# Cross-attention and quantised FFN on one core: another order of the front, and unread transposes of the identity on TensorE

## What is computed

```
x = x + Wo @ attention(q = Wq @ layernorm(x) + bq, k = Wk @ ctx + bk, v = Wv @ ctx + bv) + bo
        # scores over D x D for each head, scaled by 1/8, softmax over the last axis
x = x + (silu(h @ gate) * (h @ up)) @ down,    h = layernorm(x)
        # gate, up: 512 x 1792, down: 1792 x 512, each (int - zero) * scale by groups of 128 rows
```

## Time and profile before

| | us |
|---|---|
| median of 3 runs | 454.9 (454.37 to 455.94) |
| the profiled execution | 455.48 |
| its span in the trace | 453.7 |
| first `gate_up` starts at | 55.88 of the span |
| PE / DVE / ACT / POOL busy | 408.0 / 326.9 / 332.7 / 269.4 |

### The profile page before, as it was taken

One profiled execution on the slowest core, in us unless ns is written; L12 is line 12 of the kernel. 1 busy time (PEld: TensorE's weight loads), 2 busy tenths in 40 slices (PEclk: granted clock), 3 DMA queues, 4 the chain that ended last, 5 costly groups with the idle time before them and its releaser, 6 DMA issues.

```text
span 453.7 us, 10637 instructions
## 1 busy us (share of the span) xinstructions
PE 408.0 (90%) x4178; PEld 318.2 (70%) x4178; DVE 326.9 (72%) x581; ACT 332.7 (73%) x538; POOL 269.4 (59%) x264
## 2 busy tenths in 40 slices
PE   3566598899798799999999989999999999999994
PEld 2544365677575577777787777877778888888873
DVE  2857623899687776878887756877877666666676
ACT  2135579788687678877867958877878999888970
POOL 3263387779859665666555655656556555555561
PEclk9998579999999999999999989999999999999998
DMA  5985243768374100000201000000000000000003
GB/s 176 360 297 174 93 125 102 255 206 259 128 232 140 62 2 9 17 25 2 73 25 48 0 1 25 2 25 1 25 26 24 0 1 1 23 25 23 24 1 92
DMA packets 27139, 35.50 MB, mean 78 GB/s; under 512 B 2218, under 2 KB 18770, under 8 KB 27090
## 3 DMA queue, kind: packets, MB, share of 16 engines
q1 hardware_dynamic: 26642, 34.76, 23.2%
q10 hardware_dynamic: 320, 0.07, 0.1%
q0 software_dynamic: 128, 0.00, 0.0%
HBM read 30.63 MB, written 4.19 MB: 77 GB/s over the span
## 4 chain that ended last, share of the span: by engine, by line
PE 66%; POOL 11%; issue 9%; DVE 7%; ACT 4%; DMA 2%; SPq 0%; POOLq 0%; DVEq 0%; ACTq 0%
PE banks L708 19%; PE banks L710 17%; PE banks L721 9%; PE banks L722 9%; PE banks L612 3%; POOL t_sb L406 3%; POOL hr L419 2%; PE banks L630 2%; DVE yT L933 2%; PE banks L622 2%; DMA x_sb<-in_x 2%; POOL hr L415 1%; PE banks L641 1%; PE banks L652 1%; ACT banks L529 1%
## 5 line engine op out<-in xcount | busy, mean ns | idle before, releaser
L529 ACT ACTIVATE banks<-banks,ratio 128x512 f32<-128x512 f32 x336 | 208.5, 665 | 37.6 <-PE banks L710 26.8
L708 PE MATMUL banks<-xT,wgu 128*128 128x512 f32 x448 | 184.0, 411 | 5.1 <-DVE t_sb L918 2.7
L933 DVE SCALAR_TENSOR_TENSOR yT<-banks,sd,yT 128x512 f32<-128x512 f32 x208 | 154.5, 747 | 45.7 <-PE banks L722 45.4
L710 PE MATMUL banks<-xT,wgu 128*128 128x512 f32 x448 | 176.6, 394 | 0.0
L406 POOL TENSOR_TENSOR t_sb<-t_sb,u_sb 128x512 f32<-128x512 f32 x56 | 72.9, 1302 | 94.4 <-DVE t_sb L918 94.2
L708 PEld LDWEIGHTS banks<-xT,wgu 128*128 128x128 f32 x448 | 85.2, 190 | 27.5 <-issue 2.9
L721 PE MATMUL banks<-hr,wd 128*128 128x512 f32 x224 | 90.0, 402 | 9.0 <-DVE yT L933 5.6
L710 PEld LDWEIGHTS banks<-xT,wgu 128*128 128x128 f32 x448 | 85.3, 190 | 15.5
L722 PE MATMUL banks<-hr,wd 128*128 128x512 f32 x224 | 87.9, 393 | 0.0
L419 POOL TENSOR_TENSOR hr<-t_sb,hr 128x512 fp32r<-128x512 f32 x56 | 72.1, 1288 | 5.1 <-ACT hr L551 0.7
L721 PEld LDWEIGHTS banks<-hr,wd 128*128 128x128 f32 x224 | 42.2, 188 | 25.2 <-DVE yT L933 13.3
(11 more groups left out here) (80 smaller groups left out, 376.9 us busy)
## 6 DMA issues: line engine op xcount, KB each, us to landing
x_sb<-in_x SPq DMA_DIRECT2D x16, 256.0 KB, 5.4
out<-x_sb SPq DMA_DIRECT2D x16, 256.0 KB, 2.3
wgu_in<-in_L_ffn_gate_w SPq DMA_DIRECT2D x7, 512.0 KB, 6.7
z_in<-in_L_ffn_gate_z SPq DMA_DIRECT2D x7, 512.0 KB, 4.7
wgu_in<-in_L_ffn_up_w SPq DMA_DIRECT2D x7, 512.0 KB, 6.4
z_in<-in_L_ffn_up_z SPq DMA_DIRECT2D x7, 512.0 KB, 4.6
wd_in<-in_L_ffn_down_w SPq DMA_DIRECT2D x7, 512.0 KB, 5.5
z_in<-in_L_ffn_down_z SPq DMA_DIRECT2D x7, 512.0 KB, 4.3
```

Source lines behind the costliest of these rows:

```text
L529: act.activation(banks[:, bank, :], banks[:, bank, :], ACT.Copy, scale=ratio[:, m, g, it:it + 1]).then_inc(done[n % 2], 1)
L708: pe.matmul(banks[:, bank, :], w, xT[:, c % 2, 0, g, :], start=g == 0, stop=False, skip_group_check=True)
L710: pe.matmul(banks[:, bank, :], w, xT[:, c % 2, 1, g, :], start=False, stop=True, skip_group_check=True).then_inc(full[n % 2], 1)
L933: dve.scalar_tensor_tensor(y, bank, sd[:, it, b:b + 1], y, ALU.mult, ALU.add).then_inc(s_free, 1)
```

## The change

In the front:

- `e_sb` has two buffers, by t % 2: `less_max(t)` waits for `mix(t-2)`.
- bq and bk are loaded by POOL's queue (ahead of bv and bo) and no longer by SP's; `take_qk` reads the bias with a repeating pattern, so POOL's expansion (L425) goes.
- DVE: `stats(0,1)` stands ahead of the copy of the first weights (`take_w(0)`). `take_w(1)` and `prepare` leave the place ahead of `most(0)`: the first goes behind `take_qk(1)`, the second behind `invert(0)`; `divide` goes behind `invert(1)`. Two copies of `prepare` go to ACT, and one copy and the last three products of `divide` to POOL (`raised`, `ratios`).
- PE: the transposes of Wv, Wo and of the scales stand behind `project(1)` and not ahead of `score(0)`; `project(1)` no longer waits for `take_qk(0)`.
- ACT: `take_a(j)` stands ahead of `convert(j-1)`.
- The last tile of the front is normalised, transposed and copied in two halves of two blocks, in two PSUM banks, and the first `gate_up` step may start on the first half. The second half of `take_qk(4)` moves behind `shift(1,3)`.
- PE transposes the identity (`stir(n)`: n transposes of 128x128 into a part of a bank that nobody reads) at 19 places of the front, 140 times in all.

The core of the diff:

```diff
+            def stir(n, bank=RING_BANK + 1):
+                for _ in range(n):
+                    pe.transpose(banks[:, bank, 3 * P:4 * P], ident[:, :], ident[:, :])
+
             pe.wait_ge(s_id, 2)
+            stir(16)
             pe.wait_ge(s_wsm, 32)
...
+            stir(6)
             pe.wait_ge(s_wT, 1)
             project(0)
+            stir(12)
+            score(0)
+            project(1)
             pe.wait_ge(s_wsm2, 32)
...
-            score(0)
-            pe.wait_ge(s_qk, 2)
-            project(1)
             for j in range(PRE):
                 if j + 1 < PRE:
+                    stir(6)
                     pe.wait_ge(s_sub, j + 1)
                     score(j + 1)
...
                 else:
+                    stir(5)
                     pe.wait_ge(s_x1, j)
                 values(j)
...
+                stir(6)
                 pe.wait_ge(s_v, j + 1)
                 mix(j)
+                stir(5)
                 apply(j)
             turn_x(PRE - 2)
-            turn_x(PRE - 1)
+            stir(22)
+            pe.wait_ge(s_free, PRE - 1)
+            for h, (n, done) in enumerate(((s_lastn, s_lastX), (s_xn2, s_full))):
+                pe.wait_ge(n, (1, PRE)[h])
+                for g in range(2 * h, 2 * h + 2):
+                    mm = pe.transpose(banks[:, RING_BANK + h, g * P:(g + 1) * P],
+                                      xn2[:, (PRE - 1) % 2, g * P:(g + 1) * P], ident[:, :])
+                mm.then_inc(done, 1)
+            stir(7, U_BANK[1])
...
             def less_max(t):
                 dve.wait_ge(s_mx, t + 1)
-                if t >= 1:
-                    dve.wait_ge(s_bM, t)
+                if t >= 2:
+                    dve.wait_ge(s_bM, t - 1)
```

More of the change, by code:

```diff
@@ L169, in xattn_ffn @@
         v_sb = sb("v_sb", [P, 2, 2, 4 * Lh])
-        e_sb = sb("e_sb", [P, 2, NC, D])
+        e_sb = sb("e_sb", [P, 2, 2, NC, D])
         aT = sb("aT", [P, 2, 4 * D])
@@ L220, in xattn_ffn @@
             sem(n) for n in ("s_tanh", "s_gt", "s_uf", "s_h", "s_hi", "s_lo"))
+        s_lastn, s_lastX, s_lasthi, s_lastlo = (sem(n) for n in ("s_lastn", "s_lastX", "s_lasthi", "s_lastlo"))
         s_out = sem("s_out")
@@ L366, in _ @@
             pool.memset(power[:, :], -0.5).then_inc(s_id, 1)
+            for m, v in enumerate((bq, bk)):
+                pool.dma_start(bqk[:, m, :],
+                               v.rearrange("(a o) -> a o", a=1).partition_broadcast(P)).then_inc(s_bias, 16)
             for h in range(2):
@@ L428, in _ @@
                 weigh(j)
+                if j == 0:
+                    raised()
                 if j >= 1:
@@ L499, in power_of @@
                 act.wait_ge(s_sub, t + 1)
-                act.activation(e_sb[:, :, :, :], e_sb[:, :, :, :], ACT.Exp, scale=SCALE).then_inc(s_exp, 1)
+                act.activation(e_sb[:, t % 2, :, :, :], e_sb[:, t % 2, :, :, :], ACT.Exp, scale=SCALE).then_inc(s_exp, 1)
             def take_a(t):
@@ L559, in _ @@
                     norm1(j + 2)
+                if j == 0:
+                    act.wait_ge(s_tr, 3)
+                    ng = 2 * NG * NI
+                    act.copy(flat(sg), banks[:, 4, 0:ng]).then_inc(s_scl, 1)
+                    act.copy(sd[:, :, :].rearrange("p g c -> p (g c)"), banks[:, 4, ng:ng + NI * NC]).then_inc(s_scl, 1)
                 take_v(j)
@@ L562, in _ @@
                     take_x(j - 2)
-                if j >= 1:
+                take_a(j)
+                if 1 <= j < PRE - 1:
                     convert(j - 1)
-                take_a(j)
                 if j >= 1:
@@ L568, in _ @@
             take_x(PRE - 2)
-            norm2(PRE - 1)
-            take_x(PRE - 1)
+            convert(PRE - 2)
+            t = PRE - 1
+            act.wait_ge(s_nm[1], PRE)
+            act.wait_ge(s_full, slot["X", PRE - 3] + 1)
+            for h, done in enumerate((s_lastn, s_xn2)):
+                cols = slice(2 * h * P, (2 * h + 2) * P)
+                act.activation(xn2[:, t % 2, cols], x_sb[:, t, cols], ACT.Identity, bias=nm[:, 1, t:t + 1],
+                               scale=rs[:, 1, t:t + 1]).then_inc(done, 1)
+            for h, done in enumerate((s_lasthi, s_xhi)):
+                act.wait_ge((s_lastX, s_full)[h], (1, PRE)[h])
+                g = slice(2 * h, 2 * h + 2)
+                act.copy(xT[:, 0, 0, g, t * P:(t + 1) * P], blocks(RING_BANK + h)[:, g, :]).then_inc(done, 1)
             convert(PRE - 1)
@@ L640, in mix @@
                         h = NC * g + j
-                        mm = pe.matmul(banks[o, 6 + b, j * D:(j + 1) * D], e_sb[r, h % 2, h // 2, :], wT[r, 3, :],
+                        mm = pe.matmul(banks[o, 6 + b, j * D:(j + 1) * D], e_sb[r, t % 2, h % 2, h // 2, :], wT[r, 3, :],
                                        start=True, stop=True)
@@ L700, in gate_up @@
                         pe.wait_ge(s_sub, PRE)
+                if n == 0 and g == 2:
+                    pe.wait_ge(s_free, PRE)
                 for bank, full, done, last, m in ((G_BANK[n % 2], s_G, s_Gs, s_gt, 0),
@@ L746, in _ @@
                 for r in HALVES:
-                    mm = pe.matmul(banks[r, 5, m * D:(m + 1) * D], wraw[:, m, :], ident[0:D, 0:D], start=True, stop=True)
+                    mm = pe.matmul(banks[r, 7, m * D:(m + 1) * D], wraw[:, m, :], ident[0:D, 0:D], start=True, stop=True)
             mm.then_inc(s_tr, 1)
@@ L960, in _ @@
             stats(0, 2)
-            take_w(1)
-            prepare()
             for j in range(PRE):
@@ L976, in _ @@
                 invert(j)
+                if j == 0:
+                    prepare()
+                    dve.wait_ge(s_bvo, 64)
+                if j == 1:
+                    divide()
                 if j >= 1:
@@ L985, in _ @@
             take_qk(PRE, 0)
-            take_qk(PRE, 1)
             residual(PRE - 1)
@@ L990, in _ @@
             shift(1, PRE - 1)
-            rest_x(PRE - 1)
+            take_qk(PRE, 1)
+            for h in range(2):
+                dve.wait_ge((s_lasthi, s_xhi)[h], (1, PRE)[h])
+                g, cols = slice(2 * h, 2 * h + 2), slice((PRE - 1) * P, PRE * P)
+                dve.tensor_tensor(xT[:, 0, 1, g, cols], blocks(RING_BANK + h)[:, g, :],
+                                  xT[:, 0, 0, g, cols].bitcast(F32),
+                                  ALU.subtract).then_inc((s_lastlo, s_free)[h], 1)
             for q in range(PLACES):
```

78 lines of the change are left out of this document (38 added, 40 removed).

## The result

| | before | changed kernel |
|---|---|---|
| median, runs on the same chip | 454.63 us (10 runs, 453.67 to 457.35) | 452.81 us (10 runs, 451.23 to 453.94) |
| ratio, 95% interval | | 0.9946 [0.9923, 0.9970] |
| the profiled execution, its span | 455.48, 453.7 | 453.45, 451.6 |
| residual(0), residual(3) start at | 27.13, 49.58 | 28.78, 51.05 |
| first, second gate_up step start at | 55.88, 59.80 | 55.97, 58.12 |

The change makes the kernel faster by 0.54% by the ratio, about 2.5 us; the two medians lie 1.8 apart. Either is less than a third of the 8.3 that were forecast. In the profiled executions the front isn't shorter at all: the first gate_up starts where it did. What is won there is won behind it.

What follows compares the result with a forecast made beforehand. The bound was TensorE waiting 25 us in the front, before gate_up at 55.88. Terms of 2.7 + 2.7 + 2.6 + 1.3 = 9.3, less 2.7, plus 1.7 behind, gave 8.3 won: 454.9 to 446.6 us, range 443 to 461.5.

Steps and rivals of the forecast that it cites:

- the four terms for the front: The gains forecast ahead of the first gate_up: 2.7, 2.7, 2.6 and 1.3 us, 9.3 in all with the clock up.
- x of tile 1: Opening DMAs: without the bias loads on SP's queue tile 1's x lands at about 7.0, take_qk(0) starts 2.7 us earlier.
- my walk: Estimate of the front, engine by engine, from traced durations, without code pauses; it gave 55.2 for the old gate_up, traced 55.9.
- DVE without prepare: First tile: the FFN's scales leave the path ahead of most(0); with faster batches residual(0) is at 21.7, 2.7 us more.
- Pauses: In the front: 2.0 us taken off the gain for code pauses and a clock that rises later than 8 us.
- The third rival: Pauses for TensorE's code before gate_up eat the gain: 1.2 us won, 453.7, no change within 0.3%; chance 0.08.
- The ring from residual(0) to residual(3): Front's repeating tile steps: 19.9 us for 22.45 with two e_sb buffers and the clock up, 2.6 us won.
- The last tile in halves: From residual(3) to the first gate_up: 5.0 us for 6.3, only first halves ahead of it; 1.3 us won.
- Behind the front: First gate_up matmuls, values(4) and score(4): about 2.1 us at the higher clock, from 55.88 to 59.80 before; 1.7 us won.
- The first rival: The transposes don't lift the clock and push real batches apart: gate_up 4 to 8 us late, 461 us; chance 0.26.
- The second rival: The clock in the front comes late or in parts: gate_up at 53, 450.6 us; chance 0.13.
- The last doubt of the prediction: Gate_up starts 6 us earlier but the time doesn't follow, as a wait behind the front, on POOL or weights, takes it back.

Runs made afterwards that it cites:

- e6: Changed kernel without the loads of bq and bk, zeros in their place, so part of the computation is left out: 447.8 us, ratio 0.9832 to before.
- e10: Changed kernel with bq and bk loaded as two rows into one partition and spread by one TensorE product: 447.5 us, ratio 0.9811 to before.
- e13: Kernel before with only bq and bk as two rows, still issued by SP ahead of tile 1's x: 449.4 us, ratio 0.9842.
- e4: Changed kernel with the weights from the second piece on held back until mix(0) is done: 450.3 us, ratio 0.9897 to before.
- e11: Changed kernel with held weights, 74 unread products for the 140 transposes, and bq and bk as two rows: 446.4 us, ratio 0.9788 to before.
- e12: e11 with bv and bo loaded as rows too: 447.1 us, ratio 0.9794 to the kernel before.
- e5: Changed kernel with the 140 unread transposes replaced by 74 longer unread products, half as many instructions: 451.0 us, ratio 0.9922 to before.
- e1: Changed kernel without its 140 unread transposes: 453.9 us, ratio 1.0003 to before.
- e2: Kernel before with the 140 unread transposes added at the same waits and nothing else: 452.6 us, ratio 0.9944.
- e9: Changed kernel with only the last 29 unread transposes, behind residual(3): 452.5 us, ratio 0.9941 to before.
- e7: Kernel before with only the last 29 unread transposes added, behind residual(3): 453.6 us, ratio 0.9955.
- e8: Changed kernel with both the weights held until mix(0) and 74 unread products for the 140 transposes: 448.9 us, ratio 0.9849 to before.

## Why the prediction was right and wrong

Faster by more than 0.3% was the forecast, and 452.8 lies in the range of 443.0 to 461.5; but the size was missed by more than two thirds, and three of the four terms for the front came to nothing.

**x of tile 1, 2.7 us: this step failed first.** It took the landing between "as long as now" (8.9) and "right behind context 0" (5), at 7.0, and said that the trace didn't separate what the two broadcasts cost. The trace of before did say more than that: bk landed 0.9 us ahead of x, with the engines 0.13 to 0.30 busy from 4 to 7 us, so x was held by the loads in its queue and not by the 0.6 us that issuing each takes. What it couldn't say is what they would cost on POOL's queue. The measured 9.44 lies above even the first end, because there their packets take 28 engine-microseconds in the same 16 engines that x needs. I moved the issue in my walk, and the cost was in the transfer. Without them x is there by 5.9 to 6.6 (e6, e10, e13). My range for it, 5 to 9, didn't hold the outcome.

**DVE without prepare, 2.7 us: the mechanism worked, and was spent.** From the end of take_qk(0) to less_max(0) it is 2.5 us (14.2 to 16.68), where it was 3.7 (13.75 to 17.42). But take_qk(0) started 0.46 us later, and then the code's pause in mix(0) took 3.26 us and with it the clock: apply(0) and score(2) ran at 1.13 per batch. residual(0) was forecast at 21.7 and measured at 28.78. With the weights held it is at 25.88 (e4), with x at 5.9 as well and half the code at 21.68 (e11; 22.56 in e12, which does the same there): to come near the walk's number it takes all three.

**Pauses, allowed for with 2.0 us (2.7 less the walk's own 0.7): mis-sized.** Today's pauses stood where something else was slow too, or late in the front; the change's 140 transposes and its earlier work moved the third boundary of the code out of apply(0), where a wait had covered it, into mix(0). One pause of 3.26 us and what it did to the clock cost more than the whole allowance. The third rival, "the gain is eaten by pauses", with x still at 9 and 1.2 us won, is the nearest to what happened; I gave it 0.08. Its arithmetic was in the rows, 254 instructions a piece, and counting the matmuls of the new order up to each boundary would have put one into mix(0).

**The ring from residual(0) to residual(3), 2.6 us: failed in its own right.** It takes 22.27 us where 19.9 was forecast and 22.45 was before. In none of the kernels of the table does it come under 21.1, whatever the clock, the buffers or the code: 21.8 in e13 with one e_sb buffer at mixed levels, 22.4 in e10 with two and most batches at 0.69. less_max(1) no longer waits for mix(0), as said. What came in its place is in the chain above. First, in the turn after the pause the transposes are on the path, 1.47 us ahead of score(2) at the lower level. Then, in the next turn, ACT has convert 1.05, norm2 0.81, exp 0.62 and norm1 0.80 in a row from 36.12 to 39.10, and project(4) waits for the last: the change put take_a ahead of convert. Before, the first convert ran at 31.80 in a wait (take_a(1) still had to wait 1.39 us behind it); now it stands ahead of norm1. My walk had ACT's steps as covered. How many of the 2.4 us missing here are ACT's and how many the transposes' no run separates.

**The last tile in halves, 1.3 us: right.** 4.92 us from residual(3) to gate_up (51.05 to 55.97), 5.0 forecast, 6.3 before; 4.9 in e4, e5, e10 and e11 too. The halves and the clock share it: 5.17 with the halves and no transposes (e1), 5.84 with the clock up and no halves (e2). And the 22 transposes can take it back: in e9 the clock is still low when they start, they last 4.35 us instead of 2.56, and the way is 6.30.

**Behind the front, 1.7 us: right.** 2.15 us between the two gate_up steps, 2.1 forecast, 3.92 before. It is the larger part of the measured gain, as the ratio of e7 with 29 transposes alone bears out.

**The clock.** The transposes lift it: 0.45 us for the eight products at 6.82, 0.69 before and in e1, which is the changed kernel without them; PEclk 1.00 from 50 to 60. The first rival, 0.26 of my chances, is out. The Trainium skill's rule ("TensorE: Matmul & The Clock Gate", Part 4: PE-mode transpose), that the full clock does not engage for transposes, disagrees with this trace: sixteen transposes were all that ran ahead of the batch at 6.82. The second rival, a clock that comes in parts, did happen beside the third. It was up at 6.8, down from 8, up at 15, down at 25.1 at the end of the pause, and up from 32 on. Here 22 transposes ahead of four waits a turn were no help against a wait for a DMA or for code: the level fell around both.

**Nothing was lost behind the front.** The last doubt of the prediction, that POOL or the weights would take an earlier gate_up back, is answered by e10: gate_up starts 4.2 us earlier than in the changed kernel (51.73 against 55.97), and the median is 5.3 us lower (on another chip; the ratio is 1.35% lower, 6 us).

What stays open: how much the rearrangement of the front is worth once x and the code are in time. e10 against e13 says 0.3% (0.9811 to 0.9842) with transposes and rearrangement together, which is less than the two intervals tell apart, and no run has the rearrangement alone there. Also open is what sets the start of tile 1's statistics between 7.5 and 10.9 us while the spread loads are there, on either queue.

## What to carry over

Before a load is moved to another queue, look at when it lands and not only at what its issue costs. A stretch in which the DMA engines are nearly full and move little names the loads to reshape (the changed kernel); so does one in which they are nearly idle while a later load of the same queue waits (the kernel before). Reshaping them (a row and one product with ones) was worth more than a new order of the whole front. Count an engine's instructions up to each boundary of its code whenever a change adds instructions or lets work run earlier, and keep large transfers away from the boundaries. And test a filler alone before building on it: 29 products that nobody reads, just ahead of the first dense work, gave what 140 and a rearranged front gave.

## What the runs showed of the hardware

- A load that spreads 256 bytes over 128 partitions (32 KB written) from POOL's queue takes as much packet time as 0.9 us of all 16 DMA engines: two of them 22.5% of 8 us (20.8 to 25.8% in the six kernels that do it), against 1.2% for the rows. From SP's queue the same two take 4.0 engine-microseconds in place of 28, leave the engines 0.21 to 0.31 busy from 4 to 7 us (before, e2, e7), and still hold x behind them to 9.1 to 10.9. From POOL's queue they hold other loads as well: the products on Wq and Wk start at 5.6 to 7.4 in the six kernels that spread the biases from POOL's queue, and at 5.2 to 5.7 in all others.
- TensorE's code comes in pieces of 254 instructions, 16 KB each, and in every kernel here at least one piece was late in the front, by up to 3.3 us. TensorE goes on 1.3 to 1.5 us after the piece's transfer has ended. The pauses follow the instruction count (moved by one batch when the unread work was halved) and the traffic (gone from mix(0) and back in mix(2) when the weights were held until then).
- The granted clock rose behind sixteen transposes of the identity alone, and had fallen again at 8 us, with 1.84 us of waiting in between, though six more transposes ran from 7.20 to 8.08. Behind the same sixteen the eight products took 0.45 us in e2, e4 and e6 too; in e10, where they followed at once at 5.21, they still took 0.69, and the six transposes behind them ran at the higher level. Eight products of 128 x 512 in bf16 in their place (3.3 to 3.6 us) had lifted the clock for that batch in one kernel of four: 0.45 in e12, 0.69 in e5, e8 and e11.
